# AdaLN and MoE feed-forward kernel, last batches of the second layer: order of the products, banks and engines changed

## The chip, the cores and the metric

One Trainium2 chip, one of its cores. The metric is the device time of one execution in microseconds (us), the median of three runs: 165.51 for the kernel before. The kernel takes all inputs from HBM and writes its output there.

## What is computed

Input x is 4 batches of 256 tokens with 256 channels, float32. Two layers follow each other, each of the form x = x + ffn(cond(x)). The condition part is a bidirectional recurrence over the tokens (its keys and values come from a second input, its gate is the sigmoid of x). The first layer's feed-forward is a routed mixture of 8 experts, two per token, with a shared MLP beside it. The second layer's feed-forward, where the change lies, is small:

```python
logits = jnp.einsum('bsd,ed->bse', x, W_gate)
routing_weights, selected_experts = jax.lax.top_k(logits, TOP_K)
shared_out = jnp.einsum('bsd,od->bso', jax.nn.relu(jnp.einsum('bsd,od->bso', x, W_up)), W_down)
rw = jax.nn.softmax(routing_weights, axis=-1)
expert_out = jnp.einsum('bsd,do->bso', x, W_expert)
moe_out = jnp.sum(rw, axis=-1, keepdims=True) * expert_out
return shared_out + moe_out
```

All experts share one matrix, so per token there is one row `expert_out`, scaled by the sum of its two softmax weights. Here x is the output of the second condition part, which carries a factor per batch (`oscale` in the kernel).

## The kernel before

The kernel is written by hand for the five engines: each has its own list of instructions, and counting semaphores order them between engines. A wait stops its engine, and all that stands behind it in that engine's list. P is 128 partitions, B = 4 batches, TB = 2 tiles of 128 tokens in a batch, CH = 2 halves of 128 channels, E = 8. The tiles of tokens are numbered n = 0 to 7, two for each batch.

The first 135 us hold the recurrences of both layers (VectorE, with ScalarE and GpSimd, called POOL here), the shared MLP, the expert products, and the routing through HBM. The last 28 us are the second layer's feed-forward, a loop `for b in range(B)` on TensorE, ScalarE and VectorE. For a batch b these steps follow:

- VectorE, `combine(b)`: adds the two gathered expert rows of layer 0 to `xt`, in the pass of an earlier batch (that of batch 2 in the pass of batch 0, that of batch 3 in the pass of batch 1). TensorE, `turn_x1(b)`: turns the two tiles into bank `tp[b % 2]`. ScalarE, `tanh_x1(b)` (line 699), and VectorE, `gate_x1(b)` (line 1005), make the input `h1`. For b >= 1 the products are made of float32r parts: ScalarE writes the high part `h1_r` (`high_h1`, line 706), VectorE the low part (line 1026).
- TensorE, up products: for two output halves o, each of 2 x 3 calls (2 for b = 0), into the halves of bank `hb[b % 2]` (lines 1256 to 1266). The semaphore `up1_ready` counts one for a batch. Then `turn_x1(b + 1)`.
- TensorE, expert products: for each tile i of the batch 6 calls into `hb[2 + i]` with 264 columns, 256 of the expert row and 8 gate logits (lines 1271 to 1281). `hb[3]` is the bank named `dk`. They wait until the expert rows of the batch before are taken (`ex_taken`).
- ScalarE: relu of the whole bank to `hid1` (line 715), the turned rows' tanh and the high part of the next batch, then the tanh `dth1` of the difference of the two largest logits (line 721).
- VectorE: the maxima (line 1021) and their difference `dtop1` (line 1023).
- The expert rows. For b = 0 and 3 (`direct`) VectorE computes the weights (lines 1030 to 1032) and adds the weighted row from PSUM to `xt` (line 1040). For b = 1 and 2 ScalarE computes the weights (lines 724 to 729) and writes the weighted row to `gate_a` (line 734), and POOL adds it to `xt` (`add_expert`, line 522).
- TensorE, down products: for each tile i, over c, into `dn[i]` (lines 1287 to 1291). They wait for `hid1` and for the adds of the batch before (`y_done`). Each of these four calls is two records in the trace, as the data are plain float32.
- VectorE: the last add, from `dn[i]` to `xt` (line 1051), after which SP stores the tile (line 347).

The trace gives all products made by the helper `mm` the line 1056, so they are told apart by tile: `hb`, `dk`, `dn`, `tp`.

The order of the loop on TensorE is up, turn, experts, down for each batch. On ScalarE it is

```python
act.wait_ge(up1_ready, b + 1)
if b >= 2:
    act.wait_ge(y_ready, TB * (b - 1))
nc.scalar.activation(hid1[:, b % 2], hb[b % 2][:].rearrange("p (c t) -> p c t", c=CH), ACT.Relu,
                     scale=oscale[:, b:b + 1]).then_inc(hid1_ready, 1)
if b + 1 < B:
    tanh_x1(b + 1)
    high_h1(b + 1)
act.wait_ge(dtop1_ready, b + 1)
```

Of the kernel before, what the change touches and what calls it, by code (L numbers as in the profile page):

```python
# [47 lines left out]
STEPS = 6  # L48
STEPS0 = (4, 1, 1, 2, 0, 0, 0, 2, 1, 4, 0, 1, 2, 0, 0, 0, 0, 0, 0)
# [9 lines left out]
def adaln_ffn(nc, x_cm, x_tm, k_cm, cond, wu, router, sup, sdn, mup, mdn, l1w, out):  # L59
# [3 lines left out]
    with ExitStack() as ctx:  # L63
# [218 lines left out]
        block = ctx.enter_context(nc.Block())  # L282

# [67 lines left out]
        def _(pool):  # L351
# [182 lines left out]
            add_expert(2)  # L534
# [3 lines left out]
        def _(act):  # L538
# [170 lines left out]
            act.wait_ge(halfo_ready, 1)  # L709
            for b in range(B):  # L710
                scales(nchunks + b)
                act.wait_ge(up1_ready, b + 1)
                if b >= 2:
                    act.wait_ge(y_ready, TB * (b - 1))
                nc.scalar.activation(hid1[:, b % 2], hb[b % 2][:].rearrange("p (c t) -> p c t", c=CH), ACT.Relu,
                                     scale=oscale[:, b:b + 1]).then_inc(hid1_ready, 1)
                if b + 1 < B:
                    tanh_x1(b + 1)
                    high_h1(b + 1)
                act.wait_ge(dtop1_ready, b + 1)  # L720
                nc.scalar.activation(dth1[:, b], dtop1[:, b], ACT.Tanh, scale=halfo[:, b:b + 1]).then_inc(dth1_ready, 1)
                if 1 <= b < B - 1:
                    act.wait_ge(dth1_ready, b + 1)
                    nc.scalar.activation(rw[:, b, 0], dth1[:, b], ACT.Identity, bias=halfo[:, b:b + 1], scale=halfo[:, b:b + 1]).then_inc(rw_ready, 1)
                    nc.scalar.activation(rw[:, b, 1], dth1[:, b], ACT.Identity, bias=halfo[:, b:b + 1], scale=minus[:, b:b + 1]).then_inc(rw_ready, 1)
                    for i in range(TB):
                        if i == 0:
                            act.wait_ge(rw_ready, 4 * b - 1)
                        nc.scalar.activation(rw[:, b, 2, i:i + 1], rw[:, b, 0, i:i + 1], ACT.Identity, bias=rw[:, b, 1, i:i + 1]).then_inc(rw_ready, 1)
                    act.wait_ge(rw_ready, 4 * b + 1)  # L730
                    for i in range(TB):
                        if b >= 2:
                            act.wait_ge(ex_added, (b - 2) * TB + i + 1)
                        nc.scalar.activation(gate_a[:, i, 0:C], hb[2 + i][:, 0:C], ACT.Copy, scale=rw[:, b, 2, i:i + 1]).then_inc(ex_taken, 1)

        @block.vector
        def _(v):
            ticks = [0]

            def tick(ins):  # L740

                ticks[0] += 1
                ins.then_inc(vec, 1)
                return ticks[0]
# [262 lines left out]

            halves()
# [4 lines left out]
            for b in range(B):  # L1013
# [6 lines left out]
                for i in range(TB):  # L1020
                    n = tick(nc.vector.max(top1[:, b, i], hb[2 + i][:, C:C + E]))
# [5 lines left out]
                direct = b in (0, B - 1)  # L1027
# [7 lines left out]
                if direct:  # L1035
                    v.wait_ge(rw_ready, 1 if b == 0 else 4 * (B - 2) + 2)
                    for i in range(TB):
                        n_ = b * TB + i
                        v.wait_ge(x1_ready, n_ + 1)
                        nc.vector.scalar_tensor_tensor(out=xt[:, n_], in0=hb[2 + i][:, 0:C], scalar=rw[:, b, 2, i:i + 1],  # L1040
                                                       in1=xt[:, n_], op0=ALU.mult, op1=ALU.add).then_inc(ex_taken, 1)
                if 1 <= b < B - 2:
                    combine(b + 2)
                for i in range(TB):
                    n_ = b * TB + i
                    if direct:
                        v.wait_ge(ex_taken, n_ + 1)
                    else:
                        v.wait_ge(ex_added, n_ - TB + 1)
                    v.wait_ge(y_ready, n_ + 1)  # L1050
                    nc.vector.tensor_tensor(xt[:, n_], dn[i][:, 0:C], xt[:, n_], ALU.add).then_inc(y_done, 1)

        @block.tensor
        def _(pe):
# [191 lines left out]
            idle_products(WARM[2], hb[1])  # L1246
            for b in range(B):
# [8 lines left out]
                for o in range(CH):  # L1256
                    for c in range(CH):
                        at = c * C + o * P
                        dst = hb[b % 2][:, o * T:(o + 1) * T]
                        if b == 0:  # L1260
                            last = mm(dst, l1_s[:, at:at + P], h1[:, b % 2, c], c == 0, c == CH - 1)
                        else:
                            mm(dst, l1_r[:, 0, at:at + P], h1_r[:, b % 2, 0, c], c == 0, False)
                            mm(dst, l1_r[:, 0, at:at + P], h1_r[:, b % 2, 1, c], False, False)
                            last = mm(dst, l1_r[:, 1, at:at + P], h1_r[:, b % 2, 0, c], False, c == CH - 1)
                last.then_inc(up1_ready, 1)
                if b + 1 < B:
                    turn_x1(b + 1)
                if b >= 1:
                    pe.wait_ge(ex_taken, b * TB)  # L1270
                for i in range(TB):
                    for c in range(CH):
                        at = CH * C + c * (C + E)
                        dst, rows = hb[2 + i][:, 0:C + E], slice(i * P, (i + 1) * P)
                        if b == 0:
                            last = mm(dst, h1[:, b % 2, c, rows], l1_s[:, at:at + C + E], c == 0, c == CH - 1)
                        else:
                            mm(dst, h1_r[:, b % 2, 0, c, rows], l1_r[:, 0, at:at + C + E], c == 0, False)
                            mm(dst, h1_r[:, b % 2, 0, c, rows], l1_r[:, 1, at:at + C + E], False, False)
                            last = mm(dst, h1_r[:, b % 2, 1, c, rows], l1_r[:, 0, at:at + C + E], False, c == CH - 1)  # L1280
                last.then_inc(ex_ready, 1)
                if b >= 1:
                    pe.wait_ge(y_done, b * TB)
                else:
                    pe.wait_ge(sh_taken, B)
                pe.wait_ge(hid1_ready, b + 1)
                for i in range(TB):
# [56 lines left out]
```

## Time and profile before

| | |
|---|---|
| median of 3 runs | 165.51 us (165.51 to 165.52) |
| profiled execution, its own time | 165.76 us |
| its span (first to last instruction) | 164.0 us |
| TensorE busy | 149.4 us, 91% of the span |
| VectorE, POOL, ScalarE busy | 129.2, 103.9, 82.9 us |

A row of a timeline gives start and length in us, engine, line, operation, output and inputs, and how many instructions were merged (x18); in brackets how long the engine was idle before, and what ended the idle time. PE is TensorE, DVE VectorE, ACT ScalarE, POOL GpSimd, SP the queue that issues loads and stores. A merged row reaches from the start of its first instruction to the modelled end of its last. A weight load (PEld) has rows of its own and overlaps the products. In the chain of waits a row's length is the time for which that piece was what the end waited for.

### The profile page before, as it was taken

The numbers are of one execution on the slowest core, as the hardware profiler recorded it, in microseconds if no ns is written. First come the engines' busy times: TensorE is split into PE (matmuls) and PEld (weight loads), VectorE is DVE, ScalarE is ACT, GpSimd is POOL, SyncE is SP. The second block draws the span as 40 slices with busy tenths as digits, with TensorE's granted clock in tenths as the row PEclk, the third lists the DMA queues.
The fourth block names the chain that finished last, engine by engine and source line by source line (L and its number), as shares of the span: only waits on it lengthen the run. The fifth ranks groups of instructions, "written<-read, shape, count | busy, mean of one in ns | idle before, by whom it ended". The sixth has DMA issues, their size and how long they took to land.

```text
span 164.0 us, 2547 instructions
## 1 busy us (share of the span) xinstructions
PE 149.4 (91%) x804; PEld 131.5 (80%) x804; DVE 129.2 (79%) x287; ACT 82.9 (51%) x189; POOL 103.9 (63%) x109
## 2 busy tenths in 40 slices
PE   0296999999999999998999999999999999889991
PEld 0276888888898888886999999999988787778890
DVE  0899999979999987804979949899799564797644
ACT  3799973766071253004377743883843201537740
POOL 5384666896899777793347743665845777774230
PEclk9999999999999999999999999999999999999999
DMA  3999999998200133219902072022222233334111
GB/s 113 263 336 367 415 396 365 215 228 327 74 0 4 64 111 111 72 44 322 349 2 82 0 244 80 2 80 80 80 83 80 64 96 104 92 98 128 64 64 64
DMA packets 14844, 23.63 MB, mean 144 GB/s; under 512 B 1974, under 2 KB 10375, under 8 KB 14704
## 3 DMA queue, kind: packets, MB, share of 16 engines
q1 hardware_dynamic: 13152, 19.48, 36.9%
q0 software_dynamic: 1536, 3.99, 7.8%
q8 instruction: 6, 0.10, 0.3%
q14 instruction: 6, 0.05, 0.1%
q10 hardware_dynamic: 144, 0.00, 0.0%
HBM read 15.29 MB, written 8.39 MB: 144 GB/s over the span
## 4 chain that ended last, share of the span: by engine, by line
PE 60%; DVE 15%; POOL 11%; issue 6%; DMA 5%; ACT 1%; DVEq 0%; POOLq 0%
PE hb L1056 29%; PE dn L1056 25%; POOL buf L514 5%; POOL mup_s L514 5%; PE tp L1177 3%; DMA wu_s<-wu 2%; DMA mup_s<-slots_out,get_at 2%; PE tp L1095 2%; DVE rden L861 2%; DVE nf L772 1%; DVE df L772 1%; DMA slots_out<-outb 1%; DVE dk L823 1%; DVE ek L790 1%; PE dk L1056 1%
## 5 line engine op out<-in xcount | busy, mean ns | idle before, releaser
L1056 PE MATMUL hb<-xc,sup_s 128*128 128x256 f32 x136 | 31.3, 381 | 0.0
L621 ACT ACTIVATE gate_a<-hb 128x256 f32<-128x256 f32 (+3 forms) x38 | 15.3, 404 | 30.9 <-PE hb L1056 27.4
L1056 PEld LDWEIGHTS hb<-xc,sup_s 128*128 128x128 f32 x136 | 25.4, 190 | 3.2
L1056 PE MATMUL hb<-bufT,mup_w 128*112 128x320 f32 (+1 forms) x144 | 23.6, 317 | 0.0
L1056 PE MATMUL dn<-mdn_s,hidm 112*128 112x256 f32 x96 | 22.1, 380 | 0.0
L1056 PEld LDWEIGHTS hb<-bufT,mup_w 128*112 128x112 f32 (+1 forms) x144 | 21.4, 179 | 0.7 <-issue 0.3
L1056 PE MATMUL dn<-sdn_s,hid 128*128 128x256 f32 x96 | 21.5, 380 | 0.1
L1056 PEld LDWEIGHTS dn<-sdn_s,hid 128*128 128x128 f32 x96 | 18.2, 190 | 2.9 <-DVE hid L889 0.5
L1056 PEld LDWEIGHTS dn<-mdn_s,hidm 112*128 112x128 f32 x96 | 17.7, 190 | 2.4 <-issue 0.3
L424 POOL DMA_INDIRECT slots_in<-htok,put_at x16 | 15.9, 991 | 4.6 <-issue 4.6
L451 POOL TENSOR_TENSOR mup_w<-mup_s,mup_w 128x704 fp32r<-128x704 f32 x8 | 13.7, 1708 | 5.5 <-ACT mup_w L636 5.5
L889 DVE TENSOR_TENSOR hid<-hb,gate_a 128x256 f32<-128x256 f32 (+1 forms) x22 | 8.9, 416 | 7.7 <-ACT gate_a L621 7.6
L1056 PE MATMUL dn<-k,ident 128*128 128x256 f32 x26 | 7.8, 458 | 7.2 <-DVE df L772 7.2
L575 ACT ACTIVATE gd<-df,gain 128x255 f32<-128x255 f32 x16 | 7.9, 506 | 12.0 <-DVE df L772 11.7
L405 POOL TENSOR_TENSOR euv<-euv,nf 128x512 f32<-128x512 f32 x7 | 8.9, 1276 | 7.7 <-DVE dk L821 6.0
L398 POOL TENSOR_TENSOR euk<-euk,df 128x512 f32<-128x512 f32 x7 | 8.9, 1276 | 6.9 <-DVE df L779 6.6
L823 DVE RECIPROCAL dk<-dk 128x256 f32<-128x256 f32 x7 | 12.4, 1766 | 0.2
L1056 PEld LDWEIGHTS dn<-k,ident 128*128 128x128 f32 x26 | 6.0, 238 | 8.2 <-issue 7.1
L382 POOL TENSOR_TENSOR euv<-euk,k 128x512 f32<-128x512 f32 x8 | 10.3, 1293 | 1.0 <-DVE euk L794 1.0
L514 POOL DMA_INDIRECT mup_s<-slots_out,get_at x8 | 9.0, 1131 | 2.4 <-issue 2.4
L514 POOL DMA_INDIRECT buf<-slots_out,get_at x8 | 7.9, 992 | 4.1 <-issue 2.1
L889 DVE TENSOR_TENSOR hidm<-hb,gate_a 112x320 f32<-112x320 f32 (+1 forms) x16 | 7.6, 481 | 3.6 <-ACT gate_a L621 3.5
(148 smaller groups left out, 306.0 us busy)
## 6 DMA issues: line engine op xcount, KB each, us to landing
mup_s<-mup SPq DMA_DIRECT2D x4, 704.0 KB, 13.4
slots_in<-outb SPq DMA_DIRECT2D x10, 256.0 KB, 11.1
slots_out<-outb SPq DMA_DIRECT2D x8, 256.0 KB, 2.1
buf<-slots_in SPq DMA_DIRECT2D x4, 384.0 KB, 4.4
k<-k_cm SPq DMA_DIRECT2D x4, 256.0 KB, 4.0
xc<-x_cm SPq DMA_DIRECT2D x4, 256.0 KB, 7.0
sup_s<-sup SPq DMA_DIRECT2D x2, 512.0 KB, 7.3
xt<-x_tm SPq DMA_DIRECT2D x1, 1024.0 KB, 11.3
```

The source lines that it names most:

```text
L382: nc.gpsimd.tensor_tensor(euv[:, n % 2], euk[:, l, b], k[:, b], ALU.mult).then_inc(euv_ready, 1)
L398: nc.gpsimd.tensor_tensor(euk[:, l, b], euk[:, l, b], df[:], ALU.add).then_inc(den_summed, 1)
L405: nc.gpsimd.tensor_tensor(euv[:, n % 2], euv[:, n % 2], nf[:], ALU.add).then_inc(num_ready[n], 1)
L424: nc.gpsimd.indirect_dma_start(out=slots_in, out_offset=bass.IndirectOffsetOnAxis(ap=put_at[:, j, n:n + 1], axis=0), in_=htok[:, n], in_of ...
L451: nc.gpsimd.tensor_tensor(mup_w[:, e % 2, 1], mup_s[:, e], mup_w[:, e % 2, 0].bitcast(F32), ALU.subtract).then_inc(mup_low, 1)
L514: nc.gpsimd.indirect_dma_start(out=got_of(b, j, i), out_offset=None, in_=slots_out, in_offset=bass.IndirectOffsetOnAxis(ap=get_at[:, j, b ...
L575: nc.scalar.activation(dst[:, c, 0:T - 1], fwd[:, c, 0:T - 1], ACT.Copy, scale=gain[:, l, b, c:c + 1]).then_inc(scaled, 1)
L621: nc.scalar.activation(dst, src, ACT.Silu).then_inc(silu_ready, 1)
L823: after(tick(nc.vector.reciprocal(pair, pair)))
L889: nc.vector.tensor_tensor(dst, up, g, ALU.mult).then_inc(hid_ready, 1)
L1056: return nc.tensor.matmul(dst, w, m, start=first, stop=last)
L1177: last = nc.tensor.transpose(tp[t % 2][:, at:at + P], buf[:, q % 2, 2 * i + k_, c * P:(c + 1) * P], ident[:])
```

## The change

- Batch 3 (the last): TensorE makes the expert products first, into `tp[0]` and `tp[1]`, then the up products, each half o in a bank of its own (`hb[1]`, `hb[0]`) with a count of `up1_ready` each. ScalarE does the tanh of the logits' difference ahead of the relu, and the relu in two halves. The down products run over c outside and i inside, into `hb[2]` and `dk`; those of c wait for half c of `hid1`. They wait for the taken expert rows of batch 2 and no longer for its last adds.
- Batch 2: the weights and the weighted expert rows are done by VectorE from PSUM, as for batches 0 and 3; ScalarE's and POOL's part of it goes. VectorE's last adds of batch 2 come behind the maxima and the difference of batch 3.

```diff
+DIRECT = (0, 2, 3)
...
+        def y_bank(b, i):
+            return dn[i] if b + 1 < B else hb[2 + i]
+
+        def ex_bank(b, i):
+            return hb[2 + i] if b + 1 < B else tp[i]
...
             add_expert(1)
             behind_steps(nchunks + 2)
-            add_expert(2)
...
+            def dth_1(b):
+                act.wait_ge(dtop1_ready, b + 1)
+                nc.scalar.activation(dth1[:, b], dtop1[:, b], ACT.Tanh, scale=halfo[:, b:b + 1]).then_inc(dth1_ready, 1)
+
             for b in range(B):
                 scales(nchunks + b)
-                act.wait_ge(up1_ready, b + 1)
+                if b == B - 1:
+                    dth_1(b)
                 if b >= 2:
                     act.wait_ge(y_ready, TB * (b - 1))
-                nc.scalar.activation(hid1[:, b % 2], hb[b % 2][:].rearrange("p (c t) -> p c t", c=CH), ACT.Relu,
-                                     scale=oscale[:, b:b + 1]).then_inc(hid1_ready, 1)
+                if b + 1 < B:
+                    act.wait_ge(up1_ready, b + 1)
+                    nc.scalar.activation(hid1[:, b % 2], hb[b % 2][:].rearrange("p (c t) -> p c t", c=CH), ACT.Relu,
+                                         scale=oscale[:, b:b + 1]).then_inc(hid1_ready, 1)
+                else:
+                    for o in range(CH):
+                        act.wait_ge(up1_ready, b + 1 + o)
+                        nc.scalar.activation(hid1[:, b % 2, o], hb[1 - o][:, 0:T], ACT.Relu,
+                                             scale=oscale[:, b:b + 1]).then_inc(hid1_ready, 1)
...
-                if 1 <= b < B - 1:
+                if b + 1 < B:
+                    dth_1(b)
+                if b not in DIRECT:
...
-                        if b >= 2:
-                            act.wait_ge(ex_added, (b - 2) * TB + i + 1)
...
+            def finish(b):
+                for i in range(TB):
+                    n_ = b * TB + i
+                    if b in DIRECT:
+                        v.wait_ge(ex_taken, n_ + 1)
+                    else:
+                        v.wait_ge(ex_added, n_ - TB + 1)
+                    v.wait_ge(y_ready, n_ + 1)
+                    nc.vector.tensor_tensor(xt[:, n_], y_bank(b, i)[:, 0:C], xt[:, n_], ALU.add).then_inc(y_done, 1)
...
-                    n = tick(nc.vector.max(top1[:, b, i], hb[2 + i][:, C:C + E]))
+                    n = tick(nc.vector.max(top1[:, b, i], ex_bank(b, i)[:, C:C + E]))
...
-                direct = b in (0, B - 1)
+                if b == B - 1:
+                    finish(b - 1)
+                direct = b in DIRECT
...
-                        nc.vector.scalar_tensor_tensor(out=xt[:, n_], in0=hb[2 + i][:, 0:C], scalar=rw[:, b, 2, i:i + 1],
+                        nc.vector.scalar_tensor_tensor(out=xt[:, n_], in0=ex_bank(b, i)[:, 0:C], scalar=rw[:, b, 2, i:i + 1],
...
-                for i in range(TB):
-                    n_ = b * TB + i
-                    if direct:
-                        v.wait_ge(ex_taken, n_ + 1)
-                    else:
-                        v.wait_ge(ex_added, n_ - TB + 1)
-                    v.wait_ge(y_ready, n_ + 1)
-                    nc.vector.tensor_tensor(xt[:, n_], dn[i][:, 0:C], xt[:, n_], ALU.add).then_inc(y_done, 1)
+                if b != B - 2:
+                    finish(b)
...
+            def up1(b):
+                for o in range(CH):
+                    for c in range(CH):
+                        at = c * C + o * P
+                        dst = hb[b % 2][:, o * T:(o + 1) * T] if b + 1 < B else hb[1 - o][:, 0:T]
...
+                    if b + 1 == B and o + 1 < CH:
+                        last.then_inc(up1_ready, 1)
+                last.then_inc(up1_ready, 1)
...
                 if b + 1 < B:
+                    up1(b)
                     turn_x1(b + 1)
-                if b >= 1:
-                    pe.wait_ge(ex_taken, b * TB)
...
-                if b >= 1:
+                    if b >= 1:
+                        pe.wait_ge(ex_taken, b * TB)
+                    expert1(b)
+                else:
+                    expert1(b)
+                    up1(b)
+                if b == 0:
+                    pe.wait_ge(sh_taken, B)
+                elif b + 1 < B:
                     pe.wait_ge(y_done, b * TB)
                 else:
-                    pe.wait_ge(sh_taken, B)
+                    pe.wait_ge(ex_taken, b * TB)
+                def down1(i, c):
+                    at = L1X + c * C
+                    last = mm(y_bank(b, i)[:, 0:C], hid1[:, b % 2, c, i * P:(i + 1) * P], l1_s[:, at:at + C], c == 0, c == CH - 1)
+                    if c == CH - 1:
+                        last.then_inc(y_ready, 1)
+
                 pe.wait_ge(hid1_ready, b + 1)
-                for i in range(TB):
+                if b + 1 < B:
+                    for i in range(TB):
+                        for c in range(CH):
+                            down1(i, c)
+                else:
                     for c in range(CH):
-                        at = L1X + c * C
-                        last = mm(dn[i][:, 0:C], hid1[:, b % 2, c, i * P:(i + 1) * P], l1_s[:, at:at + C], c == 0, c == CH - 1)
-                    last.then_inc(y_ready, 1)
+                        pe.wait_ge(hid1_ready, b + 1 + c)
+                        for i in range(TB):
+                            down1(i, c)
```

`expert1(b)` holds the old loop of the expert products with `ex_bank(b, i)` as its output.

## Rows read from the trace of the kernel before

**Rows 1.** The page: span, busy time of the engines, TensorE's clock.

```profile
span 164.0 us, 2547 instructions
...
PE 149.4 (91%) x804; PEld 131.5 (80%) x804; DVE 129.2 (79%) x287; ACT 82.9 (51%) x189; POOL 103.9 (63%) x109
...
PEclk9999999999999999999999999999999999999999
```

**Rows 2.** The chain that ended last, from 155 us: start, length, what.

```profile
155.69 2.25 PE hb L1056 x18
157.94 0.74 PE dk L1056 x6
...
158.70 0.26 DVE top L1021 x2
...
161.01 0.41 DVE xt L1051
```

**Rows 3.** Timeline of TensorE's products, last 10 us.

```profile
153.80 1.89 PE L1056 MATMUL dn<-htok,hid 128*128 128x256 f32 x8
155.56 2.38 PE L1056 MATMUL hb<-bufT 128*128 128x256 f32 x18
157.78 0.89 PE L1056 MATMUL dk<-bufT 128*128 128x264 f32 x6
158.53 1.99 PE L1056 MATMUL dn<-htok,hid 128*128 128x256 f32 x8
```

**Rows 4.** Groups by line, 140 to 164 us: busy us, mean ns | idle before.

```profile
L1056 PE MATMUL dn<-htok,hid 128*128 128x256 f32 x32 | 7.7, 382 | 0.0
...
L1056 PE MATMUL hb<-bufT 128*128 128x256 f32 x36 | 5.2, 294 | 0.0
```

**Rows 5.** Timeline of VectorE, batches 2 and 3.

```profile
154.61 0.69 DVE L1026 TENSOR_TENSOR bufT<-hid,bufT 128x512 fp32r<-128x512 f32 x1 [0.17 <-ACT bufT L706]
...
158.05 0.42 DVE L1051 TENSOR_TENSOR xt<-dn,xt 128x256 f32<-128x256 f32 x1 [0.27 <-POOL xt L522]
...
158.98 0.16 DVE L1023 TENSOR_TENSOR dtop<-top 128x2 f32<-128x2 f32 x1
159.51 0.29 DVE L1030 TENSOR_SCALAR rw<-dth,halfo 128x2 f32<-128x2 f32 x1 [0.36 <-ACT dth L721]
159.70 0.28 DVE L1031 TENSOR_SCALAR rw<-dth,minus,halfo 128x2 f32<-128x2 f32 x1
160.02 0.16 DVE L1032 TENSOR_TENSOR rw<-rw 128x2 f32<-128x2 f32 x1
160.21 0.48 DVE L1040 SCALAR_TENSOR_TENSOR xt<-hb,rw,xt 128x256 f32<-128x256 f32 x1
160.62 0.47 DVE L1040 SCALAR_TENSOR_TENSOR xt<-dk,rw,xt 128x256 f32<-128x256 f32 x1
161.01 0.75 DVE L1051 TENSOR_TENSOR xt<-dn,xt 128x256 f32<-128x256 f32 x2
```

**Rows 6.** Timeline of ScalarE, batches 2 and 3.

```profile
154.49 0.29 ACT L721 ACTIVATE dth<-dtop,halfo 128x2 f32<-128x2 f32 x1
...
156.02 0.47 ACT L734 ACTIVATE gate_a<-hb,rw 128x256 f32<-128x256 f32 x1
156.40 0.47 ACT L734 ACTIVATE gate_a<-dk,rw 128x256 f32<-128x256 f32 x1
157.26 0.69 ACT L715 ACTIVATE hid<-hb,oscale 128x512 f32<-128x512 f32 x1 [0.39 <-PE hb L1056]
159.18 0.29 ACT L721 ACTIVATE dth<-dtop,halfo 128x2 f32<-128x2 f32 x1 [1.23 <-DVE dtop L1023]
```

**Rows 7.** Timeline of POOL, batch 2.

```profile
156.58 1.44 POOL L522 TENSOR_TENSOR xt<-gate_a,xt 128x256 f32<-128x256 f32 x2 [3.97 <-ACT gate_a L734]
```

**Rows 8.** The stores' line: from issue to landing.

```profile
DMA to landing us min/median/max: 1.7/1.7/2.4
```

More of the change, by code:

```diff
@@ L719, in _ @@
                     high_h1(b + 1)
-                act.wait_ge(dtop1_ready, b + 1)
-                nc.scalar.activation(dth1[:, b], dtop1[:, b], ACT.Tanh, scale=halfo[:, b:b + 1]).then_inc(dth1_ready, 1)
-                if 1 <= b < B - 1:
+                if b + 1 < B:
+                    dth_1(b)
+                if b not in DIRECT:
                     act.wait_ge(dth1_ready, b + 1)
@@ L1035, in _ @@
                 if direct:
-                    v.wait_ge(rw_ready, 1 if b == 0 else 4 * (B - 2) + 2)
+                    v.wait_ge(rw_ready, sum(1 if d in DIRECT else 4 for d in range(b + 1)))
                     for i in range(TB):
@@ L1255, in _ @@
                     pe.wait_ge(l1_low, 1)
[L1256 to L1265, printed above, removed]
@@ L1266, in _ @@
-                last.then_inc(up1_ready, 1)
                 if b + 1 < B:
+                    up1(b)
                     turn_x1(b + 1)
-                if b >= 1:
-                    pe.wait_ge(ex_taken, b * TB)
-                for i in range(TB):
[L1272 to L1280, printed above, removed]
@@ L1281, in _ @@
-                last.then_inc(ex_ready, 1)
-                if b >= 1:
+                    if b >= 1:
+                        pe.wait_ge(ex_taken, b * TB)
+                    expert1(b)
+                else:
+                    expert1(b)
+                    up1(b)
+                if b == 0:
+                    pe.wait_ge(sh_taken, B)
+                elif b + 1 < B:
                     pe.wait_ge(y_done, b * TB)
                 else:
-                    pe.wait_ge(sh_taken, B)
-                pe.wait_ge(hid1_ready, b + 1)
@@ L1287, in _ @@
-                for i in range(TB):
+                    pe.wait_ge(ex_taken, b * TB)
[4 more added lines that the diff above has]
+                        last.then_inc(y_ready, 1)
+                pe.wait_ge(hid1_ready, b + 1)
+                if b + 1 < B:
+                    for i in range(TB):
+                        for c in range(CH):
+                            down1(i, c)
+                else:
@@ L1288, in _ @@
                     for c in range(CH):
-                        at = L1X + c * C
-                        last = mm(dn[i][:, 0:C], hid1[:, b % 2, c, i * P:(i + 1) * P], l1_s[:, at:at + C], c == 0, c == CH - 1)
-                    last.then_inc(y_ready, 1)
+                        pe.wait_ge(hid1_ready, b + 1 + c)
+                        for i in range(TB):
+                            down1(i, c)
 def rev(a):
```

13 lines of the change are left out of this document (added).

## The prediction

> **What bounds the kernel now.** I read the page first, then the chain of waits, then the timelines of the last 10 us. The page has TensorE busy for 91% of a span of 164.0 us at a clock of nine tenths or more in every slice [rows 1]; so the clock is no subject here, and what matters is which engine ends last. The chain of waits answers that. Up to 158.68 us it runs through TensorE without a gap: the down products of batch 2 (`dn`), then 18 matmul records into `hb` (12 of the up products of batch 3 and 6 of its first expert rows), then 6 into `dk`. There it leaves TensorE: the maxima of the gate logits on VectorE, the weights, the weighted expert rows, the last add, and the store [rows 2]. TensorE's own last group, the down products of batch 3, begins at 158.53 and ends at 160.52 [rows 3], but the add that takes its second tile starts about 161.35. So at the end TensorE is done 0.83 us before its result is used: the bound of the last 3 us is the routing chain of batch 3, which starts only when the last expert product is done.
>
> Its length: the first maximum at 158.70, the difference at 158.98, the tanh on ScalarE at 159.18, the weights from 159.51, the weighted rows at 160.21 and 160.62, the adds at 161.01 and some 0.34 later, ended at 161.76 [rows 5, 6]. The last store and what follows it take the 2.24 us to the end of the span; a store lands 1.7 us after its issue [rows 8]. Nothing of this tail is touched.
>
> **The change, part by part.** Everything of batches 0 and 1 and of batch 2 up to its tanh keeps its order on every queue, so I hold all times up to 155.5 us fixed and rebuild only from there. The unit of the reckoning is the step between TensorE records: (2.38 - 0.29)/17 = 0.123 us in the row of 18, with 0.29 the length of one record, which its group averages; for the float32 products into `dn`, whose records average 0.38, it is (1.89 - 0.38)/7 = 0.216 us [rows 3, 4]. A reader on another engine starts 0.03 us after a group's modelled end: `dk` ends at 158.67, VectorE reads at 158.70.
>
> *Expert products of batch 3 first, in `tp`.* It removes nothing from TensorE and adds nothing: 12 expert and 12 up calls in the other order. `tp` is free: its last reader is the tanh of the turned rows of batch 3, long before. The start at 155.56 is set by the down products of batch 2 ahead of it and by the low half of `h1`, which VectorE ends at 155.30 [rows 5]; both stay. Expert products end at 155.56 + 11 x 0.123 + 0.29 = 157.20, so the maxima can start at 157.23, not 158.70: 1.47 us earlier. The first up half ends at 155.56 + 17 x 0.123 + 0.29 = 157.94, the second at 158.68.
>
> *Batch 2 on VectorE from PSUM.* ScalarE loses four small activations and two copies of 0.47 us, all that it does from the tanh's end at 154.78 to 156.87; POOL loses two adds, 1.44 us at 156.58 [rows 6, 7]. Neither was on the path of the chain, so this gives nothing of itself. VectorE gains them: weights 0.19 + 0.32 + 0.19 and two weighted rows 0.41 + 0.48 by the steps of batch 3 [rows 5], 1.59 us. They start when the low half is written (155.30; the tanh of batch 2 is done at 154.78) and end at 156.89. In the old order VectorE stood idle here, waiting for POOL, so they lie beside TensorE's products, with 0.34 us to spare before the maxima at 157.23. If that cover were gone, each further 0.1 us would move maxima, tanh and first relu together. The two plain adds of batch 2 now stand behind the difference of batch 3. The difference starts 0.28 us after the first maximum, at 157.51, and takes 0.16: the pair of adds, 0.75 us in its row, runs from 157.67 to 158.42 at the latest. It fills the wait for the tanh and overruns it: the weights would have started at 157.51 + 0.53 = 158.04 and start at 158.42. From the weights to the first last add are 1.50 us (159.51 to 161.01) [rows 5], so VectorE can add from 159.92. The stores of batch 2 are issued at about 158.0 and 158.4, as before within 0.3 us, and are gone long before the last two on SP's queue.
>
> *Tanh ahead of relu on ScalarE.* The tanh starts 0.20 us after the difference, at 157.71, and is done at 158.01. Queued behind it are both half relus, and TensorE waits for those. The first up half can be read at 157.97, so the first relu starts at about 158.03. The old relu of batch 3 took 0.69 us for 512 columns; the nearest row for 256 columns from PSUM with a scale from memory is the copy of 0.47 us, with 0.38 between starts [rows 6]. I take 0.47 (bounds: 0.38, that start step, and the whole relu's 0.69). The first half is ready at 158.50, the second, started at 158.71, at 159.18.
>
> *Down products by halves, in `hb[2]` and `dk`.* They could start at 158.53 when TensorE comes free; the first half of hid1 lets them start at 158.50 + 0.05 = 158.55 (bounds of that start 158.53 and 158.77, from the two ends above). The four records of the first half end their slots at about 159.42, and the second half is there at 159.18: no stall. The old group, which also began after a wait (for the add of tile 5, ended at 158.47), took 1.99 us and not 1.89 [rows 3, 5]; I keep 1.99. End: 160.54; tile 6 is finished 2 x 0.216 before, 160.11. The new wait for the taken rows of batch 2 is met since 156.89. It replaces the wait for the add of tile 5, which was worth under 0.02 us: TensorE was busy until 158.53 anyway.
>
> The halves are where a page speaks against the change. By the row, halving costs ScalarE 0.38 + 0.47 = 0.85 us in place of 0.69, 0.16 us, on an engine that then has nothing else. The Trainium skill, Advanced Engine Details and Errata, The Read-Write Bubble, advises large tiles of 512 or 1024 elements on ScalarE and VectorE, since each instruction exposes its latency. Kept whole by that advice, the relu would start at 158.71 and end at 159.40, the down products would run from 159.45 to 161.44, and the last add would end at 161.89: 0.13 us later than now. With the halves the sum is the one below. The trace has the dearer halves, but it also has the room for them.
>
> *Sum.* The last add waits for TensorE now: 160.54 + 0.03 = 160.57, and with its 0.42 us it ends at 160.99, against 161.76: 0.77 us earlier. VectorE, ready at 159.92, does the add of tile 6 from 160.14 to 160.55, and is free for the last. The span becomes 164.0 - 0.77 = 163.2 us. The profiled execution took 165.76 us, 1.76 around its span, and becomes 165.0. It stands 0.25 above the median of the runs, 165.51; from that median I get **164.74 us**, 0.47% less. About 0.2% (0.33 us) is what a measurement of this kernel can tell from no change. The own bounds: the shorter group of 1.89 and a release at TensorE's own 158.53 give 0.9 less, 164.6; a first half relu as long as a whole one, and a second start-up of 0.1 us at the wait between the halves, give 0.77 - 0.22 - 0.1 = 0.45 less, 165.06.
>
> **The rivals.**
> 1. *The loop through VectorE and ScalarE is late.* Maxima, difference, tanh, first relu stand in one row and TensorE's last group waits at its end; the tanh ends 0.04 us after the first up half can be read, so there is no slack behind 157.23. If the work of batch 2 on VectorE runs 0.8 us longer than I have it (0.34 of it is covered), 0.46 us of the gain is lost: 165.2. Less than that for it: the same instructions have the same lengths in batches 0 and 3. For it: two of them read `hb[2]` and `dk` while TensorE streams into `tp`, a pairing that the trace does not show; bounds for it are nothing and once again their 0.9 us.
> 2. *Slower: the same loop decides, and more.* The place is the first relu behind the tanh. The point from which it decides is a maximum started at 157.23 + 0.77 = 158.00, that is, VectorE's work of batch 2 taking 1.59 + 0.34 + 0.77 = 2.7 us. It would come so if the two weighted rows, read from PSUM beside TensorE's writes, took two and a half times their length, 2.4 us in place of 0.9: 3.1 us in all, the loop 1.16 late, 165.51 - 0.77 + 1.16 = 165.9. It could also be that the block starts late. Against it: VectorE itself completes the sums of tiles 4 and 5 in its pass of batch 0, and the tanh is done at 154.78.
> 3. *No change: VectorE's tail still ends it.* If the weights of batch 3 were held behind the adds of batch 2 so that the first last add began at 160.9, the end would stay where it is, 165.5. It needs 1.0 us on top of 159.92; the two adds wait for down products that TensorE ended at 155.69, so there is nothing to hold them.
>
> No case gives much more than forecast: TensorE's work is the same and ends near 160.5 in either order, so the last add can't start more than about 0.9 us earlier than it does.
>
> **How the numbers follow.** The forecast (end set by TensorE's last group) 0.82; rival 1 at 165.2, 0.08; rival 3, 0.04; rival 2, 0.06. Range: 164.55, the shorter group, to 165.2, which takes in its upper bound and reaches to rival 1. Faster by over 0.2% (below 165.18): 0.82 and half of rival 1, 0.86. Within 0.2%: the other half, rival 3 and a third of rival 2, 0.09. Slower by over 0.2%: 0.05.
>
> **What the changed profile would show.** Maxima of batch 3 on `tp` at about 157.2; weighted rows of batch 2 on VectorE at 155.9 and 156.3 and no add of POOL in batch 2; the adds of batch 2 between difference and weights; two relus of 0.47 at 158.0 and 158.7; down products from 158.55 to 160.5 without an inner gap; the last add waiting for TensorE at 160.6, and a chain that goes through TensorE to the end. I am wrong if TensorE idles more than 0.1 us before its last group, if the last add does not wait for it, or if anything before 155.5 us moves.

## The result, and the profile after

The changed kernel runs in 164.95 us (median of 8, 164.56 to 165.12) against 165.51 for the kernel before (median of 8, 165.42 to 166.08): a ratio of 0.9956, 95% interval 0.9936 to 0.9977. (The ratios and their intervals are worked out from the single runs; the quotient of the two medians is 0.9966.) The forecast was 164.74 with a range of 164.55 to 165.2. The profiled execution took 165.06 us for a span of 163.3, against 165.76 and 164.0.

The chain of waits, from batch 3's first product (start, length, what):

```profile
155.69 1.55 PE tp L1078 x12
157.24 1.41 PE hb L1078 x12
158.66 0.01 issue
158.67 0.67 PE hb L1078 x2
159.34 0.43 PE dk L1078 x2
159.77 0.45 PE hb L1078 x2
160.21 0.03 issue
160.24 0.02 DVEq L1031
160.26 0.04 issue
160.31 0.39 DVE xt L1032
160.69 0.04 issue
160.74 0.42 DVE xt L1032
```

Where it left TensorE at 158.68 before [rows 2], it now stays there for the expert products (`tp`), both up halves (`hb`), and six of the eight records of the down products; then come the two last adds. The maxima, tanh and weights are no longer in it. The chain puts the last add behind the add before it, but what it waits for is TensorE: the two adds start 0.43 us apart, like TensorE's pairs of records (160.04 - 159.60 = 0.44), and the last one starts 0.11 us after TensorE's last record. Where such adds have nothing to wait for they start 0.33 us apart (the kernel with the tanh last, below). TensorE's timeline gives the starts to set beside [rows 3]:

```profile
155.55 1.69 PE L1078 MATMUL tp<-bufT 128*128 128x264 f32 x12
157.08 1.58 PE L1078 MATMUL hb<-bufT 128*128 128x256 f32 x12
158.67 0.67 PE L1078 MATMUL hb<-htok,hid 128*128 128x256 f32 x2
159.17 0.59 PE L1078 MATMUL dk<-htok,hid 128*128 128x256 f32 x2
159.60 0.59 PE L1078 MATMUL hb<-htok,hid 128*128 128x256 f32 x2
160.04 0.59 PE L1078 MATMUL dk<-htok,hid 128*128 128x256 f32 x2
```

Batch 3 begins at 155.55, before it was 155.56. The code ahead of it is the same, but that the two traces agree so well is partly luck: single executions differ here (see below). The last group ends at 160.63 against 160.52, and yet the kernel is faster, as its results are taken at once. VectorE's timeline shows how (beside [rows 5]):

```profile
155.92 0.48 DVE L1068 SCALAR_TENSOR_TENSOR xt<-hb,rw,xt 128x256 f32<-128x256 f32 x1
156.32 0.48 DVE L1068 SCALAR_TENSOR_TENSOR xt<-dk,rw,xt 128x256 f32<-128x256 f32 x1
157.28 0.25 DVE L1047 MAX8 top<-tp 128x8 f32<-128x8 f32 x2 [0.48 <-PE tp L1078]
157.56 0.16 DVE L1049 TENSOR_TENSOR dtop<-top 128x2 f32<-128x2 f32 x1
157.64 0.76 DVE L1032 TENSOR_TENSOR xt<-dn,xt 128x256 f32<-128x256 f32 x2
158.31 0.28 DVE L1058 TENSOR_SCALAR rw<-dth,halfo 128x2 f32<-128x2 f32 x1
...
159.02 0.88 DVE L1068 SCALAR_TENSOR_TENSOR xt<-tp,rw,xt 128x256 f32<-128x256 f32 x2
160.31 0.42 DVE L1032 TENSOR_TENSOR xt<-hb,xt 128x256 f32<-128x256 f32 x1 [0.42 <-PE hb L1078]
160.74 0.42 DVE L1032 TENSOR_TENSOR xt<-dk,xt 128x256 f32<-128x256 f32 x1
```

The rows of batch 2 (first two) lie in time in which VectorE had waited for POOL (155.30 to 157.35 in the kernel before), and its plain adds (157.64) in the wait for the tanh. VectorE is still idle for 0.48 us before the maxima and for 0.42 before the last two adds. ScalarE's rows, beside [rows 6]:

```profile
157.76 0.30 ACT L718 ACTIVATE dth<-dtop,halfo 128x2 f32<-128x2 f32 x1 [2.98 <-DVE dtop L1049]
158.05 0.47 ACT L733 ACTIVATE hid<-hb,oscale 128x256 f32<-128x256 f32 x1
158.69 0.47 ACT L733 ACTIVATE hid<-hb,oscale 128x256 f32<-128x256 f32 x1 [0.17 <-PE hb L1078]
```

The end of the execution came 0.10 us earlier still, for a reason of SP's queue. The store of tile 7, the last, is these rows, before and after:

```profile
161.83 0.43 SPq L347 DMA_DIRECT2D out<-xt  x1
161.19 0.38 SPq L354 DMA_DIRECT2D out<-xt  x1
```

Before, the last two adds ended 0.34 us apart, and the queue, held from 161.45 to 161.78 by the store of tile 6, began the last store 0.07 us after the last add's end (161.76) and took 0.43 us for it. Now the adds are 0.43 us apart, and it begins 0.03 us after it (161.16) and takes 0.38. From the last add's end to the end of the span are 2.24 us before and 2.14 after.

### The profile page after: what moved, and what is told of

Its sections match the earlier page's. It is cut to its first block, busy times and chain, and to the rows that moved or that the text cites. A ratio compares the mean times of both kernels' runs of the same rounds, so it can differ in the third digit from the quotient of the medians.

```text
span 163.3 us, 2545 instructions
## 1 busy us (share of the span) xinstructions
PE 149.6 (92%) x804; PEld 131.6 (81%) x804; DVE 130.6 (80%) x292; ACT 81.1 (50%) x184; POOL 102.4 (63%) x107
## 4 chain that ended last, share of the span: by engine, by line
PE 62%; DVE 14%; POOL 11%; issue 5%; DMA 5%; ACT 1%; POOLq 0%; DVEq 0%
PE hb L1078 29%; PE dn L1078 25%; POOL buf L521 5%; POOL mup_s L521 5%; PE tp L1199 3%; DMA mup_s<-slots_out,get_at 2%; DMA wu_s<-wu 2%; PE tp L1117 2%; PE tp L1078 2%; DVE rden L877 2%; DVE nf L788 1%; DVE df L788 1%; DMA slots_out<-outb 1%; DVE dk L839 1%; DVE ek L806 1%
```

## The experiments

Single executions differ in when batch 3 begins (155.2 to 156.2 us in the traces), for a reason that two of the experiments look at. So the traces are compared by their **last stage**: from the first TensorE record of batch 3 to the end of the last add. It is 161.76 - 155.56 = 6.20 us in the kernel before and 161.16 - 155.55 = 5.61 in the changed one. Each is read from one trace; the changed kernel's two traces agree to 0.01 us. What follows the last add is not in it. Line numbers shift a little from kernel to kernel.

| kernel | last stage, us | median, us | kernel before, same chip | ratio, 95% interval |
|---|---|---|---|---|
| changed | 5.61 | 164.95 | 165.51 | 0.9956 (0.9936 to 0.9977) |
| changed, again | 5.61 | 165.04 | 165.71 | 0.9968 (0.9950 to 0.9987) |
| batch 2 on VectorE only | 6.21 | 165.75 | 165.81 | 0.9991 (0.9966 to 1.0016) |
| order only | 5.80 | 165.24 | 165.81 | 0.9959 (0.9937 to 0.9982) |
| whole relu | 6.53 | 166.07 | 165.81 | 1.0009 (0.9985 to 1.0033) |
| experts last | 6.41 | 165.96 | 165.81 | 1.0007 (0.9985 to 1.0029) |
| tanh last | 6.10 | 165.66, one run | 165.62 | |
| tanh between | 5.62 | 165.17 | 165.62 | 0.9977 (0.9957 to 0.9997) |
| adds before maxima | 5.61 | 164.92, one run | 165.71 | |
| two POOL adds beside | 5.61 | 164.94, one run | 165.62 | |
| one long POOL add beside | 5.97 | 165.32, one run | 165.71 | |
| POOL's adds of batch 1 later | 5.61 | 164.74 | 165.62 | 0.9951 (0.9932 to 0.9970) |
| the same, again | 5.62 | 164.90 | 165.71 | 0.9946 (0.9926 to 0.9965) |

The theory was that the order of batch 3 gives the gain, and that halves and the early tanh are what makes the order pay; the rival, that taking batch 2 off ScalarE and POOL gives it.

### Batch 2 on VectorE, alone

```diff
-            add_expert(2)
...
-                if 1 <= b < B - 1:
+                if b == 1:
...
-                direct = b in (0, B - 1)
+                direct = b != 1
```

> The kernel before with batch 2's weights and expert rows on VectorE alone; order, banks and relu as before. My theory: the last maxima still wait for the last expert product, so the first maximum of batch 3 stays at about 158.7 us and the last add ends at about 161.7: 165.5 us, ratio 0.999 to 1.001. Rival (moving the rows off ScalarE and POOL gives the gain, by freeing the last products from the adds of batch 2): 165.0 or less.

The last stage is 6.21 us, the first maximum 3.15 us after the stage's start (158.77 for 155.62; it was 158.70 for 155.56), and the interval of the ratio includes 1. The median, 165.75, is above the 165.5 forecast, as the kernel before has 165.81 on this chip. By itself this part gives nothing that can be seen; the rival falls.

### The order, with batch 2 on ScalarE and POOL

```diff
-DIRECT = (0, 2, 3)
+DIRECT = (0, 3)
...
             behind_steps(nchunks + 2)
+            add_expert(2)
```

and the wait for `ex_added` ahead of `gate_a` as before.

> The changed kernel with batch 2's expert rows back on ScalarE and POOL. My theory: VectorE's two adds of batch 2 then wait for POOL's, which end near 158.0, so they end near 158.5 in place of 158.4, the weights of batch 3 can be used by about 160.0, and the last add ends within 0.2 us of the changed kernel's 161.16: 164.9 to 165.1 us. Rival (the move to VectorE carries the gain): 165.4 or more.

The median of 165.24 us misses the forecast of 164.9 to 165.1, but that was made from a kernel before at 165.51, and on this chip it has 165.81. It lies 0.57 us below it, and the ratio (0.9959) can't be told from the changed kernel's 0.9956 and 0.9968, so the order, with the halves and the early tanh, carries most of the gain: 0.40 of 0.59 us by the last stage in the traces. In the trace the stage is 0.19 us longer than the changed kernel's, about as much as allowed, but not for the cause expected (the late adds of batch 2, which VectorE took at 158.10 without waiting). The difference of the maxima takes 0.46 us in place of 0.16, and ends as POOL's two adds end. VectorE's row in its timeline:

```profile
157.72 0.46 DVE L1052 TENSOR_TENSOR dtop<-top 128x2 f32<-128x2 f32 x1
```

and POOL's:

```profile
156.72 1.44 POOL L529 TENSOR_TENSOR xt<-gate_a,xt 128x256 f32<-128x256 f32 x2 [3.97 <-ACT gate_a L753]
```

Tanh and first relu follow it, and TensorE's last group starts at 159.01, 3.30 us after the stage's start in place of 3.12.

### The relu whole

```diff
-                        dst = hb[b % 2][:, o * T:(o + 1) * T] if b + 1 < B else hb[1 - o][:, 0:T]
+                        dst = hb[b % 2][:, o * T:(o + 1) * T]
```

and one count of `up1_ready`, one relu of 512 columns, one wait for `hid1`.

> The changed kernel with the relu of batch 3 whole: both up halves in one bank, one relu of 512 columns. My theory: relu from 158.7 to 159.4, last TensorE group starts about 159.5 in place of 158.67, last add ends about 162.0: 0.8 to 0.9 us slower than the changed kernel, 165.7 to 165.9 us, slower than the kernel before. Rival (the halves are not needed, fewer instructions are better): 164.9 or less.

The relu in ScalarE's timeline:

```profile
158.59 0.69 ACT L728 ACTIVATE hid<-hb,oscale 128x512 f32<-128x512 f32 x1 [0.70 <-PE hb L1073]
```

and the first products of the last group in TensorE's:

```profile
159.42 0.67 PE L1073 MATMUL hb<-htok,hid 128*128 128x256 f32 x2 [0.93 <-DVE xt L1063]
```

TensorE stands idle for 0.93 us, the stage is 0.92 us longer than the changed kernel's and 0.33 longer than that of the kernel before. The releaser named in the bracket had nothing to do with it; the relu ends at 159.28. The median of 166.07 us lies above the forecast of 165.7 to 165.9, on a chip where the kernel before has 165.81; against that kernel the runs show no difference (1 lies in the interval), and the 0.33 us stand in the trace alone. The whole gain hangs on the halves. This kernel also puts both up halves back into one bank; whether halves would work as well from one bank, and the expert products as well in their old banks, was not tested.

### Expert products last again

```diff
                 else:
-                    expert1(b)
                     up1(b)
+                    expert1(b)
```

and both half relus ahead of the tanh. VectorE's timeline, where batch 3's last gathered rows are added, is shown below the expectation.

> The changed kernel with the up products of batch 3 ahead of its expert products again, and the two half relus ahead of the tanh; free banks, halves and batch 2 on VectorE stay. My theory: the maxima wait for the last expert product again, first maximum about 158.8, last add ends 161.7 to 161.9: 165.4 to 165.7 us, all of the gain gone. Rival (banks and halves carry the gain): 165.1 or less.

The stage is 6.41 us, 0.21 more than before the change: the maxima come 3.14 us after the stage's start, and now batch 2's adds stand between the difference and the weights (159.70 to 160.46). The ratio has 1 in its interval: all of the gain is gone. The median, 165.96, is above the 165.4 to 165.7 forecast, again beside 165.81 for the kernel before. The add's end of 162.61 us lies beyond the forecast of 161.9, since this execution's batch 3 began 0.65 us late:

```profile
150.83 0.95 DVE L1011 SCALAR_TENSOR_TENSOR xt<-mup_s,cw,xt 128x256 f32<-128x256 f32 x1 [0.67 <-DMA mup_s<-slots_out,get_at]
151.82 0.83 DVE L1013 SCALAR_TENSOR_TENSOR xt<-mup_s,cw,xt 128x256 f32<-128x256 f32 x1
```

These are the last two adds of gathered rows, those of batch 3's second tile. Elsewhere such an instruction takes 0.48 us; here POOL's adds of batch 1 run from 150.77 for 1.60 us.

### The tanh's place

Behind both half relus, and between them:

```diff
-                if b == B - 1:
-                    dth_1(b)
...
                         nc.scalar.activation(hid1[:, b % 2, o], hb[1 - o][:, 0:T], ACT.Relu,
                                              scale=oscale[:, b:b + 1]).then_inc(hid1_ready, 1)
+                    dth_1(b)
```

(in the second kernel, `dth_1(b)` stands inside the loop over o, for o == 0).

> The changed kernel with the tanh of batch 3 behind both half relus. Theory: relus at 157.95 and 158.7, tanh about 159.1 in place of 157.76, weights of batch 3 from 159.45, and VectorE's tail sets the end again: last add ends about 6.1 us after the first expert product, in place of 5.61, some 0.5 us lost. Rival (VectorE's tail has room): 5.6 us or less.

> The changed kernel with the tanh of batch 3 between the two half relus. Theory: the first relu starts when its up half is done, about 0.1 us earlier, TensorE's last group starts at once with its idle 0.1 us gone; the weights start about 0.35 us later and are just in time: last add ends 5.5 us after the first expert product, 0 to 0.1 us less than the changed kernel. Rival (VectorE's tail then decides): 5.6 to 5.8 us.

Tanh last: the stage is 6.10 us, as expected; its chain leaves TensorE at 158.68 for the second relu, the tanh and the weights. VectorE is late here, so its last two adds have nothing to wait for:

```profile
160.90 0.41 DVE L1031 TENSOR_TENSOR xt<-hb,xt 128x256 f32<-128x256 f32 x1
161.23 0.41 DVE L1031 TENSOR_TENSOR xt<-dk,xt 128x256 f32<-128x256 f32 x1
```

Tanh between: 5.62, no gain, a miss against the 5.5 forecast. The number falls into the rival's range, but VectorE's tail does not decide here: the last add starts at 160.51, 0.10 us after TensorE's last record (159.81 + 0.60), and 0.43 after the add before it. The first relu starts 157.82 - 155.31 = 2.51 us after the stage's start, in the changed kernel 158.05 - 155.55 = 2.50, though here nothing stood ahead of it. So it is the up half that sets its start, not the tanh, and the 0.1 us that this kernel was to win was not there. Its median, 165.17, lies above the changed kernel's 164.95 and 165.04 on other chips, with single runs from 164.6 to 166.3; that says nothing of the last stage, where the two agree to 0.01 us.

### Batch 2's adds ahead of the maxima

```diff
-                if b == B - 1:
-                    finish(b - 1)
...
-                if b != B - 2:
-                    finish(b)
+                finish(b)
```

> The changed kernel with VectorE's two adds of batch 2 in their old place, ahead of the maxima of batch 3. Theory (maxima, difference, tanh and first relu stand in one row with TensorE's last group at its end, and 0.44 us are free before the maxima for 0.76 us of adds): maxima 0.3 us later, last add 5.9 us after the first expert product in place of 5.61. Rival (TensorE alone sets the end): 5.6 us.

A miss: 5.61 us, as the rival had it. VectorE began the adds at 156.55 and the maxima at 157.21, 1.82 us after the stage's start in place of 1.73, where I had expected 0.3 late. The two adds hold VectorE for 0.66 us, the two starts, not for their row of 0.74, and VectorE is free 0.39 us after the start of the last weighted row and not only at its end. Of the 0.09 us left, the first relu saw nothing: it started 0.21 us after the tanh (157.89 after 157.68), in the changed kernel 0.29 after it, as it waited for the up half.

### POOL beside VectorE's difference

```diff
+            pool.wait_ge(ex_taken, 3 * TB)
+            for i in range(2):
+                nc.gpsimd.tensor_tensor(nf[:, i], df[:, i], nf[:, i], ALU.add).then_inc(ex_added, 1)
             behind_steps(nchunks + 3)
```

> The changed kernel, and POOL makes two adds of scratch data (128 x 256, as its adds of batch 2 were) when VectorE has taken the expert rows of batch 2, near 156.8 us. Theory: POOL's adds hold up VectorE's instructions whose two inputs both lie in on-chip SBUF memory; the difference of batch 3's maxima is one, so it takes about 0.45 us in place of 0.16, tanh, relu and TensorE's last group start some 0.3 us later, and the last add ends 5.9 us after the first expert product of batch 3 in place of 5.61. Rival (the 0.46 us difference in the kernel with batch 2 on ScalarE and POOL had another cause, as its late ScalarE copies): difference 0.16 us, last add 5.6 us after the first expert product.

5.61 us, the difference took 0.16. That looks like the rival, but the timing does not let it decide: POOL's pair ran from 156.72 to 158.18, the first add 0.73 us long, to 157.45, the second 0.77, from 157.41, and the difference started at 157.42, where one follows the other. So the experiment was made again with one add of 512 columns (`nf[:], df[:], nf[:]`), which has no gap:

> As the kernel with two scratch adds on POOL beside batch 3's maxima, with one scratch add of 128 x 512 in their place, so that no gap between two adds lets VectorE through: it runs from about 1.3 to 2.6 us after the first expert product. Theory (an add of POOL holds up VectorE's instruction with two SBUF inputs for as long as it runs): the difference of the maxima, due 2.0 us after the first expert product, ends with POOL's add at 2.6, 0.4 to 0.5 us late; tanh, first relu and TensorE's last group follow, and the last add ends 6.0 to 6.1 us after the first expert product, in place of 5.61. Rival (no collision): 5.61.

VectorE's timeline:

```profile
157.15 0.25 DVE L1049 MAX8 top<-tp 128x8 f32<-128x8 f32 x2 [0.49 <-PE tp L1080]
157.43 0.62 DVE L1051 TENSOR_TENSOR dtop<-top 128x2 f32<-128x2 f32 x1
157.98 0.74 DVE L1034 TENSOR_TENSOR xt<-dn,xt 128x256 f32<-128x256 f32 x2
```

and POOL's:

```profile
156.74 1.29 POOL L542 TENSOR_TENSOR nf<-df,nf 128x512 f32<-128x512 f32 x1 [4.01 <-DVE xt L1070]
```

The difference ends at 158.05, POOL's add at 158.03. The maxima, whose input is in PSUM, keep their 0.25 us under the same add. TensorE's last group starts at 158.89, 0.35 us later in its stage than in the changed kernel, and the stage is 5.97 us, for 6.0 to 6.1 forecast. The theory holds, and it tells what batch 2 on VectorE is worth once the order is changed: it takes POOL away from beside the difference. The Trainium skill, SBUF — State Buffer, Who interferes with whom, has it as a rule that a VectorE instruction with two SBUF inputs contends with a GpSimd instruction that reads SBUF; the trace agrees, 0.62 us in place of 0.16.

### POOL's adds of batch 1 held back

The same collision stands in the kernel before and in the changed one, on the path: the last gathered row of batch 3, which TensorE waits for to turn it, takes 0.89 us and 0.84 us (lines 998 and 1014) while POOL adds batch 1's rows.

```diff
             def add_expert(b):
+                pool.wait_ge(x1_ready, NT)
...
                     gate_x1(b + 1)
+                if b == B - 2:
+                    finish(b - 1, (1,))
```

where `finish(1)` after the pass of batch 1 is for its first tile alone, and the down products of batch 2 wait for each tile's `y_done` by itself.

> The changed kernel with POOL's adds of batch 1 held until VectorE has added the last gathered rows (batch 3's), the last add of batch 1's second tile behind the gate of batch 3, and TensorE's down products of batch 2 waiting for each tile's bank by itself. Theory: POOL's adds no longer lie beside the gathered rows' adds, so the last of these takes 0.48 us in place of 0.84, and all behind it comes about 0.35 us earlier: 0.3 us less than the changed kernel in the median, and its runs lie closer together, since the collision depends on when the gathered rows land. Rival (the work pushed behind the gate collides there, or holds the down products of batch 2): no gain, or up to 0.3 us lost.

> The changed kernel itself, beside the other kernels of this call on one chip. Theory (its last stage gains 0.6 us from the first expert product of batch 3 to the last add, and its runs spread with the landing of the gathered rows and POOL's collision in batch 1): median 0.5 to 0.7 us below the kernel before, spread of half a microsecond or more; in its trace, last add 5.6 us after the first expert product of batch 3 (5.61), wherever that product starts.

> The kernel with POOL's adds of batch 1 held back, on one chip with the changed kernel. Theory (the collision of POOL's adds with the last gathered rows costs 0.35 us whenever these land after 150.5 us): median 0.2 to 0.4 us below the changed kernel. Rival (TensorE's products of batch 2 bound that stage anyway, or the move only shifts the collision): within 0.1 us of it.

The changed kernel again did as forecast: 0.67 us below the kernel before by the medians, runs over 1.39 us, a last stage of 5.61. From its trace, VectorE's rows:

```profile
150.69 0.48 DVE L1012 SCALAR_TENSOR_TENSOR xt<-mup_s,cw,xt 128x256 f32<-128x256 f32 x1 [0.39 <-DMA mup_s<-slots_out,get_at]
151.21 0.84 DVE L1014 SCALAR_TENSOR_TENSOR xt<-mup_s,cw,xt 128x256 f32<-128x256 f32 x1
```

and from the trace of the kernel with POOL held back on the same chip:

```profile
150.48 0.48 DVE L1013 SCALAR_TENSOR_TENSOR xt<-mup_s,cw,xt 128x256 f32<-128x256 f32 x1 [0.42 <-DMA mup_s<-slots_out,get_at]
151.00 0.48 DVE L1015 SCALAR_TENSOR_TENSOR xt<-mup_s,cw,xt 128x256 f32<-128x256 f32 x1
...
152.71 0.83 DVE L1022 SCALAR_TENSOR_TENSOR hid<-hid,euk 128x512 f32<-128x512 f32 x1
```

The last row is back at 0.48 us. From the first of these rows to batch 3's first product are 155.59 - 150.69 = 4.90 us in the changed kernel and 155.17 - 150.48 = 4.69 with POOL held back: 0.21 saved, not 0.35. POOL's adds now run from 151.56 for 1.42 us and lie beside the gate of batch 3, which takes 0.83 us in place of 0.69; that 0.14 makes up the difference, though no run shows it by itself. In the other trace of this kernel the gathered rows landed early: VectorE took them at 150.35 without a wait, and the chain runs through TensorE's products alone up to 155.23. There batch 3 starts 4.94 us after the first of these rows, so nothing is saved.

Both forecasts for the runs are missed. On the chip that has both kernels the medians are 164.90 and 165.04, 0.14 us apart with overlapping intervals, where 0.2 to 0.4 was forecast (and 0.1 by the rival). The runs of the kernel with POOL held back spread by 0.48 us there (7 runs), those of the changed kernel by 1.39 (12), but on the other chip its spread was 1.05 (12 runs, 164.48 to 165.53). It is ahead of the kernel before on both chips; that it is faster than the changed kernel shows only in the one trace.

## Why the prediction was right

*The bound, and the order.* Right. The maxima were forecast 1.47 us earlier, at 157.23, and came at 157.28; the last add waits for TensorE, as forecast, and the chain stays there up to the two last adds. The expert products' step is (1.69 - 0.29)/11 = 0.127 us and not 0.123: they have 264 columns, and the row of 18 was mostly up products with 256. That is the 0.05.

*Batch 2 on VectorE.* The costs were right: weighted rows at 155.92 and 156.32 for 155.9 and 156.3. "Neither was on the path of the chain, so this gives nothing of itself" is shown by the part alone, 6.21 us against 6.20. What the prediction missed is what it gives with the new order: 0.19 us of last stage, the stall of VectorE behind POOL's adds. The cover of 0.34 us ahead of the maxima was called too small: the idle time is 0.48, and the adds of batch 2 put there delayed the maxima by 0.09 only.

*Tanh ahead of relu.* The times were right: tanh at 157.76 for 157.71, relus at 158.05 and 158.69 for 158.03 and 158.71. Put last, it costs 6.10 - 5.61 = 0.49 us; but it need not stand ahead of both relus, as between them the stage is the same. The sentence that there is no slack behind 157.23 was nearly true for the tanh: the first relu could have started 0.09 us earlier behind it (0.29 after the tanh's start, where 0.21 was seen elsewhere).

*Halves.* Right: the whole relu gives a stage of 6.53 us, 0.33 more than before the change, where 0.13 more was forecast; the median agrees only in sign (ratio 1.0009, 1 within its interval). The Trainium skill, Advanced Engine Details and Errata, The Read-Write Bubble, advises large tiles on ScalarE. For the engine's own time the traces agree: two halves back to back take 0.82 us (with the long POOL add), the whole relu 0.69. For the stage they do not bear it out, as the large tile costs 0.92 us there.

*Down products, and the sum.* Here two terms were too small, both the time between one engine's end and the next one's start. First relu to TensorE: taken 0.05 us, measured 0.15 (158.52 to 158.67). TensorE's float32 group to VectorE: taken 0.03, measured 0.11 (160.63 to 160.74). The first relu was 0.02 late and the group 0.03 shorter than taken (1.96 for 1.99). Together 0.10 + 0.08 + 0.02 - 0.03 = 0.17 us: 161.16 in place of 160.99.

The 0.10 also touches one of the signs of being wrong, TensorE idle for more than 0.1 us before its last group. The profile counts 0.01 us, from the modelled end of the up products at 158.66. But records of products that follow without a wait start 0.14 us ahead of that modelled end (158.53 against 158.67 before the change), so by the prediction's own reckoning TensorE was idle for 0.15 us. The sign came, by 0.05 us; the mechanism stands.

In the sum these errors partly cancel with one on the other side. "Nothing of this tail is touched" was wrong: the tail behind the last add became 0.10 us shorter, as the last two stores no longer stand close in SP's queue. So the profiled execution took 165.06 us, only 0.07 more than the 164.99 reckoned. The other 0.14 us of the 0.21 between 164.74 and 164.95 come from the step to the median: the profiled execution of the kernel before stood 0.25 us above its median, that of the changed kernel 0.11. Which execution is profiled is chance, so how close the forecast came is in part luck, either way.

The chances do not quite follow from their parts: within 0.2% they give 0.04 + 0.04 + 0.02 = 0.10 and not 0.09, slower 0.04 and not 0.05. Nothing hangs on it.

*Rivals.* None came: VectorE's reads of `hb[2]` and `dk` beside TensorE's writes into `tp` took their usual 0.48 us each. But rival 1's loop is real where something holds VectorE up by more than its slack: with one long POOL add the difference came 0.46 us late, and the stage grew by 0.36.

## What to carry to other kernels

When an engine ends its work well before its last result is used, look for the short chain that starts behind its last product, and issue that product first; then check that the work now last has its own consumer cut fine enough to start before it is complete. Here the two belong together: each without the other gained nothing in the runs, and lost 0.2 to 0.3 us of the last stage in the trace. And read the length of a small instruction against its usual one: a 0.16 us difference that takes 0.46 is a collision, and work on an engine off the path can be what makes it.

## What was not expected of the hardware

- A VectorE instruction of 2 columns with both inputs in SBUF took 0.62 us under one POOL add of 512 columns, 0.46 under the second of two POOL adds of 256, and 0.16 when it started where one such add followed the other. Instructions of VectorE with an input in PSUM kept their length (maxima 0.25, adds 0.41).
- The start of TensorE's products after a ScalarE instruction they wait for came 0.14 to 0.15 us after its end (158.52 to 158.67 in the changed kernel, 159.28 to 159.42 with the whole relu, 158.87 to 159.01 with the order only); the turning of a tile came 0.04 us after the VectorE add it waits for (152.02 to 152.06). That is not a rule for VectorE: where the down products of batch 2 were done early, batch 3's first product started 0.26 us after the low half of `h1` (155.03 to 155.29, 154.91 to 155.17, with POOL held back).
- What differs between the traces lies ahead of batch 3. In the seven traces with a last stage of 5.61 or 5.62 us the time of the execution less the start of batch 3 is 109.51 to 109.54 us, while that start runs from 155.17 to 155.59. In most traces the last gathered rows set it: they landed between 150.36 and 150.81 us, since their wait was 3.3 to 3.8 us in the chains and its start moved too (146.79 to 147.27). Where they landed last both adds of them met POOL's (0.95 and 0.83 us in place of 0.48), which put batch 3 off by 0.65 us in the one trace that shows it. That the single runs without a trace spread for the same reason is not shown.
